# A decoder's state-space scan on one core: who adds the partial sums, products without use, and where the next stage is prepared

## The chip, the cores and the metric

One core of one Trainium2 chip runs the whole program. The metric is the device time of the program in microseconds, as the median of several runs; a profiled execution of the same program gives the trace.

## The reference

The reference is four layers of a decoder over 8 batches of 256 tokens with 128 features. Each layer is attention of some kind, cross attention to a context, and a feed-forward network, each followed by `x = layernorm(x + f(x))`. The change touches two of these twelve stages: the feed-forward network of the second layer (called L1f), and the stage behind it, the state-space model of the third layer (L2a).

L1f is a gated network with dequantised weights:

```
gate = silu(x @ w_gate.T);  up = x @ w_up.T;  y = (gate * up) @ w_down.T
```

L2a, for N = 16 states per feature, computes B and C (16 numbers per token each) and a step size dt (one number per token and feature) from x, and then

```
dt = softplus((x @ W_dt1 + b_dt1) @ W_dt2 + b_dt2)
h[t] = exp(dt[t] * A) * h[t-1] + (the inputs made from x[t] and B[t])
y[t] = sum over the 16 states n of C[t, n] * h[t, n]  + D * x[t]
```

## The kernel before, in words

The program is written by hand for five engines: each engine's instructions stand in one queue in the order of the code, and semaphores join the queues. Nothing reorders them. The functions below are written once per engine; a function named `scan_...` belongs to L2a, wherever it is called.

**The scan (L2a).** The 16 states of a batch are cut into four chunks of four states, so 8 batches give 32 chunks, t = 0 to 31; c = t % 4 is the chunk of a batch. A chunk is 128 features by 4 x 256 tokens. For chunk t:

- ScalarE and GpSimd (`scan_scaled`, GpSimd's line L886) scale the rows of x by B; TensorE (`scan_inputs`, L1891, 8 products) turns and spreads them into PSUM; ScalarE copies the start values over them (`start`, L2636). `scan_inputs(t)` waits until the scan of chunk t-2 has read that bank.
- ScalarE makes the decays (L2626).
- VectorE scans along the tokens (L3524) and multiplies the result in place by C (L3528), which TensorE has spread into PSUM (`spread_c`, L1977). The multiply releases the semaphore `L2a_hc`.
- TensorE (`summed`, L1989) adds the four states of the chunk by four float32 products with the identity into one PSUM bank. For c = 0 a product with the diagonal D comes first (L1987). The scan of chunk t+2 waits for `summed(t)`, since it writes the same tile.

TensorE's loop over t does, in this order: `spread_c(t)`, `summed(t-1)`, then the parts that prepare a later batch or finish an earlier one, then `scan_inputs(t+2)`. The parts are: for t % 4 = 0 `scan_project` (L1870); for 1 `scan_step_sizes` (L1877, L1879); for 2 `result` (L2008) and `cross` (L2000); for 3 `scan_turn_x` (L1859 to L1864). VectorE's loop does the norm of a finished batch (L3554, t % 4 = 0), the softplus (L3451, L3452, t % 4 = 1), scan and multiply of chunk t, then reads y (L3540), `scan_crossed_rows` (L3400, L3402, t % 4 = 0), `scan_sized` (L3410), the series of a logarithm (L3419, L3422; three steps for t % 4 = 3, two for 0) and the statistics of the layer norm (L3545, L3548, t % 4 = 3). GpSimd's loop does `scan_scaled(t+3)`, the first state of a batch (L907, L909), `scan_signed` (L895, L896), and `root` (L918, L919), which gives the rstd that VectorE's norm waits for.

**The gated network (L1f)** runs over b = 0 to 7: two wide products (`gated_widen`, L1915), SiLU on ScalarE (L2591), VectorE's product (L3466), the narrow product (`gated_narrow`, L1925), residual and statistics on VectorE (L3471, L2807 to L2812), rstd and normalised rows on GpSimd (L740, L1054). Between the batches stand pieces that prepare batches 0 and 1 of the scan: VectorE's `scan_constants` for b = 2, which ends with the table SEL of 64 x 2048 elements (L3441) and then releases ScalarE's `scan_projected(0)`; TensorE's `scan_step_sizes(0)` for b = 3 and `scan_step_sizes(1)` for b = 6. The latter waits for VectorE's `scan_crossed_rows(1)`, which stands behind two steps of the series and the softplus. ScalarE's `scan_small_exponential(1)` waits for `scan_sized(1)`.

## Time and profile before

| | us |
|---|---|
| median of 3 runs | 1726.93 |
| lowest and highest of the 3 | 1718.28, 1728.19 |
| the profiled execution's own time | 1728.67 |
| its span, first to last instruction | 1726.8 |
| mean granted TensorE clock | 0.942 |

The span is 1.9 us shorter than the profiled execution's time; the rest lies ahead of the first and behind the last instruction. The scan takes the stretch from about 775 to 958 us of the span, the gated network the one from about 718 to 775.

### The profile page before, as it was taken

What the parts mean: (1) busy time and instruction counts of PE and PEld (TensorE: products, weight loads), DVE (VectorE), ACT (ScalarE), POOL (GpSimd) and SP (SyncE); (2) the same over time, 40 slices, a digit from 0 to 9 for tenths busy, and PEclk for the clock granted to TensorE, in tenths of its full rate; (3) what the DMA queues carried; (4) which work ended last, traced back from release to release, by engine and by line L of the source; (5) the groups of instructions that cost most, each with busy time, mean ns of one, the idle gap of its engine ahead of it and who ended that gap; (6) DMA issues with size and microseconds to landing.
All of it is one profiled execution on the core that took longest, in us unless ns stands there. A gap on an engine that the chain in (4) does not pass through costs nothing.

```text
span 1726.8 us, 34149 instructions
## 1 busy us (share of the span) xinstructions
PE 1509.5 (87%) x12661; PEld 1083.3 (63%) x12661; DVE 1231.5 (71%) x2790; ACT 997.9 (58%) x2035; POOL 594.2 (34%) x800
## 2 busy tenths in 40 slices
PE   6588878789998898789999899998889999989975
PEld 5344436678787555567788667665549984755542
DVE  1688864697776798447888577758844448659888
ACT  4499943367666577356766255547754443157765
POOL 2455535578887021342222223220001111511223
PEclk9799979899999999989999999999988999799985
DMA  3200121200000000000000100000000000000000
GB/s 134 112 14 13 38 93 37 63 10 2 1 1 1 2 2 2 8 14 25 1 1 1 59 2 2 2 13 2 2 2 1 1 10 1 1 19 2 2 1 25
DMA packets 14788, 31.08 MB, mean 18 GB/s; under 512 B 1537, under 2 KB 10017, under 8 KB 13857
## 3 DMA queue, kind: packets, MB, share of 16 engines
q1 hardware_dynamic: 13602, 26.81, 4.5%
q0 software_dynamic: 1024, 2.10, 0.4%
q8 instruction: 103, 1.69, 0.4%
q14 instruction: 59, 0.48, 0.1%
HBM read 22.60 MB, written 6.29 MB: 17 GB/s over the span
## 4 chain that ended last, share of the span: by engine, by line
PE 49%; DVE 13%; POOL 13%; issue 12%; ACT 11%; DMA 1%; SPq 0%; POOLq 0%; DVEq 0%; ACTq 0%
PE PS L1488 5%; PE PS L1541 4%; POOL big L866 4%; ACT big L2361 4%; PE PS L1813 3%; DVE negmax L2938 3%; PE PS L1802 3%; POOL big L854 3%; PE PS L1891 3%; ACT big L2339 2%; PE PS L1989 2%; PE PS L1563 2%; POOL big L862 2%; PE PS L1391 2%; PE PS L1467 2%
## 5 line engine op out<-in xcount | busy, mean ns | idle before, releaser
L2339 ACT ACTIVATE big<-PS 128x1024 f32<-128x1024 f32 (+1 forms) x256 | 249.3, 974 | 157.4 <-PE PS L1495 156.9
L2938 DVE TENSOR_REDUCE negmax<-PS 128x4 f32<-128x1024 f32 x192 | 234.8, 1223 | 57.6 <-PE PS L1488 52.9
L1488 PE MATMUL PS<-KS,QS 32*128 32x256 f32 (+1 forms) x1152 | 133.4, 316 | 33.5 <-DVE negmax L2938 21.0
L1488 PEld LDWEIGHTS PS<-KS,QS 32*128 32x128 f32 x1152 | 87.3, 186 | 106.7 <-ACT big L2339 76.1
L740 POOL TENSOR_TENSOR rstd<-veps,mhalf 128x2 f32<-128x2 f32 x72 | 51.4, 714 | 249.5 <-DVE veps L2812 240.0
L1495 PE MATMUL PS<-QS,KS 32*128 32x256 f32 (+1 forms) x1152 | 133.8, 319 | 1.4 <-ACT big L2339 1.4
L1541 PE MATMUL PS<-big,V 128*32 128x256 f32 (+1 forms) x2048 | 133.6, 379 | 0.3 <-DVE V L3030 0.3
L766 POOL TENSOR_TENSOR res<-resb,XB 128x256 f32<-128x256 f32 x24 | 17.4, 727 | 254.7 <-ACT resb L2425 254.7
L2957 DVE SCALAR_TENSOR_TENSOR QT<-PS,wint 128x1024 f32<-128x1024 f32 x64 | 77.3, 1220 | 17.7 <-PE PS L1433 17.0
L808 POOL TENSOR_SCALAR KT<-QT 128x1024 f32<-128x1024 f32 x64 | 66.6, 1040 | 66.5 <-DVE QT L2957 63.3
L1495 PEld LDWEIGHTS PS<-QS,KS 32*128 32x128 f32 x1152 | 84.7, 187 | 5.5 <-issue 3.7
L2516 ACT ACTIVATE QT<-PS,W 128x256 f32<-128x256 f32 x128 | 53.6, 470 | 55.8 <-PE PS L1802 55.8
L854 POOL TENSOR_SCALAR big<-big,rsum 128x256 f32<-128x256 f32 (+1 forms) x144 | 60.7, 433 | 71.2 <-DVE rsum L2859 70.9
L1537 PE MATMUL PS<-big,V 128*32 128x512 f32 x512 | 64.5, 622 | 22.9 <-ACT big L2361 15.4
L866 POOL TENSOR_TENSOR big<-big 128x512 f32<-128x512 f32 x64 | 81.3, 1270 | 5.0
L1541 PEld LDWEIGHTS PS<-big,V 128*32 128x32 f32 x2048 | 54.2, 110 | 44.1 <-issue 15.4
L1195 PE MATMUL PS<-OT,W 128*128 128x256 f32 x272 | 75.6, 400 | 6.1 <-ACT QT L2287 6.1
L2361 ACT ACTIVATE big<-KT,W 128x1024 f32<-128x1024 f32 x64 | 73.0, 1141 | 9.0 <-POOL KT L808 9.0
L2287 ACT COPY QT<-PS 64x256 f32<-64x256 f32 x128 | 46.8, 366 | 53.4 <-DVE big L2843 51.7
L3524 DVE TENSOR_TENSOR_SCAN V<-big,PS 128x1024 f32<-128x1024 f32 x32 | 73.0, 2281 | 2.9 <-ACT PS L2636 2.4
L2361 ACT ACTIVATE big<-QT,W 128x1024 f32<-128x1024 f32 x64 | 72.8, 1138 | 2.9 <-DVE QT L2957 2.9
L1891 PE MATMUL PS<-W,QT 128*128 128x128 f32 x480 | 62.8, 286 | 9.1 <-DVE V L3524 9.1
(498 smaller groups left out, 4086.4 us busy)
## 6 DMA issues: line engine op xcount, KB each, us to landing
W<-in_wpack SPq DMA_DIRECT2D x1, 4180.0 KB, 14.0
W<-in_wpack SPq DMA_DIRECT2D x1, 2560.0 KB, 8.7
W<-in_wpack SPq DMA_DIRECT2D x1, 2449.5 KB, 9.3
y_rows<-one_more SPq DMA_DIRECT2D x1, 2048.0 KB, 9.4
masks<-in_mask SPq DMA_DIRECT2D x8, 256.0 KB, 2.9
x_rows<-x_tok SPq DMA_DIRECT2D x16, 128.0 KB, 2.0
W<-in_wpack SPq DMA_DIRECT2D x1, 1538.0 KB, 6.4
x_tok<-in_x SPq DMA_DIRECT2D x1, 1024.0 KB, 4.8
```

Source lines behind the costliest of these rows:

```text
L854: ins = nc.gpsimd.tensor_scalar(PRW[:, u % 4, c0:c1], PRW[:, u % 4, c0:c1], rsum[:, u % 16, j:j + 1], 1.0, ALU.mult, ALU.mult)
L866: nc.gpsimd.tensor_tensor(q, q, RTW[:, u % 4, :, :], ALU.add).then_inc(sem("t_rope"), 1)
L1195: mm = nc.tensor.matmul(PS[:, QKB[u % 2], k * S:(k + 1) * S], w(f"{n}_w{x}", h * P, (h + 1) * P), OT[:, b, :], start=True, stop=True)
L1488: mm = nc.tensor.matmul(PS[:, MAXB[half], o], QS[r, bm % 2, tm, j * P:(j + 1) * P], KS[r, bm % 2, tm, k], start=not a.causal, stop=last)
L1495: mm = nc.tensor.matmul(PS[:, exp_banks(ge)[half], o], KS[r, be % 2, te, kb * P:(kb + 1) * P], QS[r, be % 2, te, q], start=not a.causal, s ...
L1541: mm = nc.tensor.matmul(out_rows[:, skip:S], v, PX[:, T % 2, h, kb * S:(kb + 1) * S - skip], start=first, stop=last)
L1891: mm = nc.tensor.matmul(PS[:, bank, first:first + P], chunk("x", t)[:, (k % 2 * 4 + k // 2) * P:(k % 2 * 4 + k // 2 + 1) * P], w("L2a_ahea ...
L2339: nc.scalar.activation(PX[:, T % 2, 2 * p:2 * p + 2, 0:cols], PS[:, exp_banks(g)[0]:exp_banks(g)[0] + 2, 0:cols], ACT.Exp, scale=a.scale). ...
L2361: nc.scalar.activation((PX, PX2)[k][:, T % 2, 2 * p:2 * p + 2, :], clipped((QT, KT)[k], g), ACT.Exp, scale=a.scale, bias=w(("high_base", " ...
L2938: ins = nc.vector.tensor_reduce(negmax[:, h:h + 2, :].rearrange("p h j -> p (h j)"), banks.rearrange("p h (j k) -> p (h j) k", j=2), AX.X, ...
L2957: nc.vector.scalar_tensor_tensor(clipped(QT, g), PS[:, pair_banks(g):pair_banks(g) + 2, :], -100.0 / a.scale, capT[:, g // PAIRS % 2, :].u ...
L3524: nc.vector.tensor_tensor_scan(h, chunk("decay", t), flat(PS[:, bank:bank + 2, :]), 0.0, ALU.mult, ALU.add)\
```

## The change

There are three parts.

1. **Sums.** After its multiply, chunk t is no longer summed by four products. GpSimd adds the second half of the chunk (two states) to the first (`scan_pairs`, a tensor_tensor of 128 x 512 float32), and TensorE's `summed` has two products in place of four. `summed(t-1)` waits for GpSimd's add, and stands behind the preparing parts in TensorE's loop, just ahead of `scan_inputs(t+2)`. For c = 0 it begins with a bfloat16 product of the identity (128 x 256) that writes the unused half of the bank.
2. **Products without use.** `scan_inputs(t)` begins, for t >= 2 except t % 4 = 2, with eight bfloat16 products of 128 x 256 whose result nobody reads, ahead of its waits.
3. **Preparation.** The table SEL is built for b = 4 of the gated network in place of b = 2. The step sizes of batch 1, and what follows from them, go behind the network's own last work on TensorE, VectorE and GpSimd; `scan_crossed_rows(1)` goes ahead of the series for b = 6. GpSimd's `scan_scaled(0)` and `(1)` go behind its rows of b = 5 and b = 6.

The diff (a line of "..." stands where lines are left out):

```
+            def scan_pairs(t):
+
+                pool.wait_ge(sem("L2a_hc"), t + 1)
+                h = chunk("h", t)
+                nc.gpsimd.tensor_tensor(h[:, 0:512], h[:, 0:512], h[:, 512:1024], ALU.add).then_inc(sem("L2a_added"), 1)
...
                     if (b := due(t, SCAN_U, 4)) is not None and b >= 2:
                         scan_signed(b)
+                    if 0 <= t < 4 * B:
+                        scan_pairs(t)
                     if (b := due(t, SCAN_STATS, 4)) is not None and b < B - 1:
                         root(b)
...
                     elif b == 3:
                         scan_signed(0)
-                    elif b == 6:
-                        scan_signed(1)
-                        scan_scaled(0)
-                        scan_scaled(1)
                     inverse_root(n, b)
...
                     ins.then_inc(x_done, 1)
+                    if b in (5, 6):
+                        scan_scaled(b - 5)
+                scan_signed(1)
...
             def scan_inputs(t):
 
+                for _ in range(8 if t >= 2 and t % 4 != 2 else 0):
+                    nc.tensor.matmul(PS[:, 6, S:2 * S], identb[:, :], identb[:, :].unsqueeze(1).broadcast_to([P, 2, P]),
+                                     start=False, stop=False)
                 pe.wait_ge(sem("L2a_xs"), t + 1)
...
-                    elif b in (3, 6):
-                        scan_step_sizes(b // 6)
+                    elif b == 3:
+                        scan_step_sizes(0)
                 pe.wait_ge(sem(f"{n}_silu"), B)
                 scan_inputs(0)
                 gated_narrow(B - 1)
+                scan_step_sizes(1)
                 scan_inputs(1)
...
                 def summed(t):
                     b, c = t // 4, t % 4
-                    pe.wait_ge(sem(f"{n}_hc"), t + 1)
+                    pe.wait_ge(sem(f"{n}_added"), t + 1)
                     if c == 0:
                         if b:
                             pe.wait_ge(sem(f"{n}_y_read"), 2 * b)
-                        nc.tensor.matmul(PS[:, YB, 0:S], diag, xN(b), start=True, stop=False)
-                    for k in range(4):
+                        nc.tensor.matmul(PS[:, YB, S:2 * S], identb[:, :], identb[:, :].unsqueeze(1).broadcast_to([P, 2, P]),
+                                         start=True, stop=False)
+                        nc.tensor.matmul(PS[:, YB, 0:S], diag, xN(b), start=False, stop=False)
+                    for k in range(2):
                         mm = nc.tensor.matmul(PS[:, YB, 0:S], ident, chunk("h", t)[:, k * S:(k + 1) * S],
-                                              start=False, stop=c == 3 and k == 3)
+                                              start=False, stop=c == 3 and k == 1)
...
                     if 0 < t < 4 * B:
                         spread_c(t)
-                    if t:
-                        summed(t - 1)
...
                         scan_turn_x((t + 9) // 4)
+                    if t:
+                        summed(t - 1)
                     if t + 2 < 4 * B:
                         scan_inputs(t + 2)
...
-                line.did(nc.vector.tensor_tensor(SEL[:, :, :], inverse_parts.unsqueeze(1).broadcast_to([64, 16, P]),
-                                                 w("L2a_state", rows=64).unsqueeze(2).broadcast_to([64, 16, P]), ALU.mult))
...
+            def scan_spread():
+                line.wait()
+                line.did(nc.vector.tensor_tensor(SEL[:, :, :], inverse_parts.unsqueeze(1).broadcast_to([64, 16, P]),
+                                                 w("L2a_state", rows=64).unsqueeze(2).broadcast_to([64, 16, P]), ALU.mult))
...
+                    elif b == 4:
+                        scan_spread()
                     elif b == 5:
                         scan_series(0, 0, 3)
                     elif b == 6:
+                        scan_crossed_rows(1)
                         scan_series(0, 3, 5)
                         scan_softplus(0)
-                        scan_crossed_rows(1)
-                        scan_sized(1)
                 gated_residual(B - 1)
+                scan_sized(1)
```

In the printed order below, the lines are those of each kernel's own file: from `scan_pairs` on, the changed file's numbers are higher.

TensorE at the end of the gated network, before: wide products L1915, narrow products L1925, step sizes of batch 1 L1877 and L1879, inputs of the scan L1891.

```order
L1915 MATMUL PS<-QT,big 128x256 x3
L1877 MATMUL PS<-OT,W 128x256
L1879 MATMUL PS<-W,KT 128x16 x2
L1915 MATMUL PS<-QT,big 128x256 x3
L1925 MATMUL PS<-big,QT 128x128 x6
L1915 MATMUL PS<-QT,big 128x256 x3
L1891 MATMUL PS<-W,V 128x128 x8
L1925 MATMUL PS<-big,QT 128x128 x6
L1891 MATMUL PS<-W,V 128x128 x8
```

The same place after; the wide products are L1925, the narrow ones L1935, the step sizes L1884 and L1886, the inputs L1901.

```order
L1925 MATMUL PS<-QT,big 128x256 x6
L1935 MATMUL PS<-big,QT 128x128 x6
L1925 MATMUL PS<-QT,big 128x256 x3
L1901 MATMUL PS<-W,V 128x128 x8
L1935 MATMUL PS<-big,QT 128x128 x6
L1884 MATMUL PS<-OT,W 128x256
L1886 MATMUL PS<-W,KT 128x16 x2
L1901 MATMUL PS<-W,V 128x128 x8
```

The step sizes of batch 1 have moved from between the wide products of batches 6 and 7 to behind the last narrow product.

TensorE in the scan, the iterations t = 1 and 2, before: spreading C is L1977, the diagonal L1987, the sums L1989.

```order
L1977 MATMUL PS<-KS,SEL 128x256 x4
L1987 MATMUL PS<-KT 128x256
L1989 MATMUL PS<-V,W 128x256 x4
L1877 MATMUL PS<-OT,W 128x256
L1879 MATMUL PS<-W,KT 128x16 x2
L1891 MATMUL PS<-W,QT 128x128 x8
L1977 MATMUL PS<-KS,SEL 128x256 x4
L1989 MATMUL PS<-V,W 128x256 x4
L2000 MATMUL PS<-one_more,W 128x256
L1891 MATMUL PS<-W,QT 128x128 x8
```

After, from t = 1 to the inputs issued in t = 2: spreading C is L1988, the diagonal L2000, the sums L2002, the products without use L1893 and L1998, the cross product L2013.

```order
L1988 MATMUL PS<-KS,SEL 128x256 x4
L1884 MATMUL PS<-OT,W 128x256
L1886 MATMUL PS<-W,KT 128x16 x2
L1998 MATMUL PS<-identb 128x256
L2000 MATMUL PS<-KT 128x256
L2002 MATMUL PS<-V,W 128x256 x2
L1893 MATMUL PS<-identb 128x256 x8
L1901 MATMUL PS<-W,QT 128x128 x8
L1988 MATMUL PS<-KS,SEL 128x256 x4
L2013 MATMUL PS<-one_more,W 128x256
L2002 MATMUL PS<-V,W 128x256 x2
L1893 MATMUL PS<-identb 128x256 x8
```

The sums have half their products and stand behind the step sizes or the cross product; eight products without use stand between them and the inputs.

GpSimd in the scan, from the first state of batch 2 on (t = 6), before: first state L907 and L909, signed B L895 and L896, scaled rows L886, the root L918 and L919.

```order
L907 TENSOR_TENSOR KT<-KT 128x16
L909 TENSOR_TENSOR KT<-KT 128x16
L895 TENSOR_SCALAR rsum<-rt,W 128x16
L896 TENSOR_TENSOR sums<-rt,W 2x32
L886 TENSOR_TENSOR QT<-x_tok,rt 128x512
L918 TENSOR_SCALAR veps<-mv 128x2
L919 TENSOR_TENSOR rstd<-veps,mhalf 128x2
L886 TENSOR_TENSOR QT<-x_tok,rt 128x512 x3
```

After, from the same place: the same in lines L913 and L915, L901 and L902, L886, L924 and L925; the new adds are L895.

```order
L913 TENSOR_TENSOR KT<-KT 128x16
L915 TENSOR_TENSOR KT<-KT 128x16
L901 TENSOR_SCALAR rsum<-rt,W 128x16
L902 TENSOR_TENSOR sums<-rt,W 2x32
L895 TENSOR_TENSOR V<-V 128x512
L886 TENSOR_TENSOR QT<-x_tok,rt 128x512
L895 TENSOR_TENSOR V<-V 128x512
L924 TENSOR_SCALAR veps<-mv 128x2
L925 TENSOR_TENSOR rstd<-veps,mhalf 128x2
L886 TENSOR_TENSOR QT<-x_tok,rt 128x512
L895 TENSOR_TENSOR V<-V 128x512
L886 TENSOR_TENSOR QT<-x_tok,rt 128x512
```

An add stands behind every step's scaled rows, and for t % 4 = 3 ahead of the root that VectorE's norm waits for.

## Rows read from the trace of the kernel before

**Rows 1.** Busy time by stretch: length, five engines' busy us, PEclk, DMA share, GB/s.
```profile
754.20:767.00 12.80, 8.59 (x34) 7.27 (x34) 5.30 (x16) 4.73 (x12) 5.19 (x7) 0.73 0.01 1
...
785.00:796.00 11.00, 11.00 (x51) 8.78 (x51) 7.17 (x6) 5.86 (x18) 2.54 (x6) 0.69 0.01 1
796.00:881.00 85.00, 80.73 (x484) 68.00 (x484) 72.00 (x92) 61.60 (x183) 20.40 (x33) 1.00 0.00 1
881.00:890.00 9.00, 8.84 (x48) 7.75 (x48) 6.51 (x7) 5.56 (x16) 1.95 (x5) 0.81 0.00 0
```
**Rows 2.** Timeline of the gated network: start us, us, engine, line, operation [idle before <-releaser].
```profile
728.91 2.28 DVE L3441 TENSOR_TENSOR SEL<-On,W 64x2048 fp32r<-64x2048 f32 x1
...
731.63 0.46 ACT L2551 ACTIVATE one_more<-PS,W 16x256 f32<-16x256 f32 x1 [8.40 <-DVEq L3445]
...
736.40 1.19 PE L1877 MATMUL PS<-OT,W 64*128 64x256 f32 x2 [4.95 <-DVE one_more L3402]
...
748.38 0.42 DVE L3471 TENSOR_TENSOR res<-PS,x_tok 128x256 f32<-128x256 f32 x1 [2.88 <-PE PS L1925]
...
758.42 1.05 PE L1877 MATMUL PS<-OT,W 64*128 64x256 f32 x2 [4.21 <-DVE one_more L3402]
...
763.93 0.47 ACT L2561 ACTIVATE KT<-PS,W 128x256 f32<-128x256 f32 x1
```
**Rows 3.** Timeline ahead of the first scan.
```profile
771.38 1.26 ACT L2583 ACTIVATE QT<-x_tok,rt 128x128 f32<-128x128 f32 x4
...
774.19 0.22 POOL L907 TENSOR_TENSOR KT<-KT 128x16 f32<-128x16 f32 x1
...
774.79 0.17 ACT L2636 COPY PS<-KT 128x8 f32<-128x8 f32 x1 [2.15 <-POOL KT L909]
...
775.16 2.29 DVE L3524 TENSOR_TENSOR_SCAN V<-big,PS 128x1024 f32<-128x1024 f32 x1 [2.38 <-ACT PS L2636]
```
**Rows 4.** Timeline of one batch of the scan.
```profile
819.41 1.22 DVE L3528 TENSOR_TENSOR V<-V,PS 128x1024 f32<-128x1024 f32 x1
...
823.81 0.61 DVE L3554 SCALAR_TENSOR_TENSOR x_tok<-res,mv,rstd 128x128 f32<-128x128 f32 x2 [1.12 <-POOL rstd L919]
...
824.33 0.73 PE L1977 MATMUL PS<-KS,SEL 64*128 64x256 f32 x4
...
828.92 0.47 DVE L3400 SCALAR_TENSOR_TENSOR KS<-PS,W,KS 32x256 fp32r<-32x256 f32 x1 [0.71 <-ACT OT L2553]
...
832.08 2.29 DVE L3524 TENSOR_TENSOR_SCAN V<-big,PS 128x1024 f32<-128x1024 f32 x1
...
834.51 2.02 PE L1891 MATMUL PS<-W,QT 128*128 128x128 f32 x16 [1.11 <-DVE V L3524]
...
836.47 0.73 PE L1977 MATMUL PS<-KS,SEL 64*128 64x256 f32 x4
...
837.13 1.99 PE L1989 MATMUL PS<-V,W 128*128 128x256 f32 x8
...
838.96 0.38 PE L2008 MATMUL PS<-W,XB 128*128 128x128 f32 x2
...
841.88 0.73 PE L1977 MATMUL PS<-KS,SEL 64*128 64x256 f32 x4
...
842.72 1.22 DVE L3528 TENSOR_TENSOR V<-V,PS 128x1024 f32<-128x1024 f32 x1
```
**Rows 5.** By line: ns min/median/max, first and last start, forms.
```profile
L1786 PE MATMUL PS<-causal,identb x40: 270/272/273, 309.5 to 313.8; 128*128 128x256 bf16 x40
...
L866 POOL TENSOR_TENSOR big<-big x64: 1260/1268/1328, 332.3 to 549.7; 128x512 f32<-128x512 f32 x64
```
**Rows 6.** VectorE's softplus by line, and its one slow case on the timeline.
```profile
L3451 DVE SCALAR_TENSOR_TENSOR OT<-OT,xs x8: 424/425/1220, 756.3 to 923.9; 128x256 f32<-128x256 f32 x8
...
923.76 1.04 POOL L886 TENSOR_TENSOR QT<-x_tok,rt 128x512 f32<-128x512 f32 x1 [3.61 <-PE PS L1891]
923.86 1.22 DVE L3451 SCALAR_TENSOR_TENSOR OT<-OT,xs 128x256 f32<-128x256 f32 x1
```

## The prediction

> **What bounds the kernel now.** I read the timeline of the stretch that the change touches, then the busy time by stretch, and then the timeline again, ahead of the scan.
>
> The scan comes first. One batch of it, four chunks, repeats every 23.3 us, and the timeline shows what holds the period [rows 4]. TensorE's iteration t % 4 = 0 begins at 824.33 with the spread of C; ScalarE, once TensorE's inputs are through, needs until 828.92 before VectorE can begin the crossed rows (it waited 0.71 for ScalarE): 4.6. From there VectorE does series and softplus and starts the scan at 832.08 (3.2), TensorE's inputs wait 1.11 for that scan and start at 834.51 (2.4), take 1.96 to the next spread at 836.47, and from there TensorE works without a pause: 5.4 to the spread at 841.88, then 5.8 to the same point of the next batch. The sum is 23.3. So TensorE is the bound in two iterations out of four, and ScalarE and VectorE are in the other two. VectorE itself has little to spare: from the end of its multiply of chunk 3 (819.41 + 1.22 = 820.63) to its next scan it needs 3.7, 1.12 of it a wait for GpSimd's rstd; only the 0.71 ahead of L3400 is slack.
>
> The clock is the second view [rows 1]. In 796 to 881 TensorE had 1.00 of its clock; in 785 to 796 it had 0.69 and in 881 to 890 0.81, with TensorE busy throughout. The first stretch follows a wait for the scan, and so does the second; each such wait is 1.1 us long, as the one at 834.51.
>
> The third view is the gated network [rows 2]. TensorE stood 4.95 us ahead of the step sizes of batch 0 at 736.40, and 4.21 us ahead of those of batch 1 at 758.42, both for VectorE's L3402. After the second it ran at 0.73 [rows 1]. The first scan at 775.16 waited for ScalarE's start copy, which had waited 2.15 for GpSimd's first state [rows 3].
>
> **The change part by part.**
>
> *The table SEL.* ScalarE's L2551 is released by VectorE's queue behind the table and one short instruction (8.40 of wait) [rows 2]. The table takes 2.28. With it gone from b = 2, the chain ScalarE, crossed rows, step sizes comes 2.3 sooner, and so does all that follows in the gated network. For b = 4 the table lies ahead of L3471 at 748.38, where VectorE idled 2.88: that hides it. Without that cover it would cost the 2.3 again. I take -2.3; bounds -2.3 and 0.
>
> *Batch 1's step sizes.* TensorE no longer stands 4.2 in the middle of the network, so the last rows are normalised sooner, and GpSimd's first state with them. What is late next is ScalarE: its queue before the first scan ended at 771.38 + 1.26 = 772.64 [rows 3]. That queue hangs on `scan_small_exponential(1)`, which still waits for the step sizes of batch 1. Before, ScalarE came to it at 763.93 [rows 2]. In the new order TensorE has, from 754.20 on, wide, narrow, wide, inputs(0), narrow and the step sizes: two wide pairs and the inputs of 1.96 [rows 4] and the rest come, as an estimate, to 8 to 9 us at full clock, and one wait for VectorE's product to about 1. That is 763.2 to 764.2, the time of before: the saved wait and the saved half clock pay for the work placed ahead. So the start copy goes from 774.79 to about 772.9: -1.9. Bounds: 0, where another wait takes its place, and -4.2, the whole wait. GpSimd's scaled rows (1.04 each) go behind rows of b = 5 and 6 and are wanted later than they end; `scan_signed(1)` lands ahead of the first state, in the 2.15 that ScalarE has to spare. Neither costs anything.
>
> *Sums and products without use.* Four sums take 838.96 - 837.13 = 1.83 [rows 4]; two take 0.92, so 0.91 is saved per chunk. A bfloat16 product of 128 x 256 comes every (313.8 - 309.5)/39 = 0.11 [rows 5]; eight take 0.88. In the iterations t % 4 = 2 and 3, which bind, one replaces the other: -0.03 each. For t % 4 = 1 the products lie in the 1.11 of wait. For t % 4 = 0 there are none, and 0.91 is saved, but the inputs wait for the scan there and the path goes by ScalarE's 4.6 anyway. The projection moves ahead of the sums, which ScalarE sees by less than 0.1. So per batch -0.1, over 6 batches -0.6; bounds -1.2 and 0. The new wait, for GpSimd's add: the add takes 1.27 [rows 5], with semaphores 1.4 behind the multiply. For t % 4 = 2 TensorE comes to its sums 1.6 after its spread began and more than 2 us behind the multiply, for 3 later still; it doesn't wait. Queued behind the waiting sums are only the useless products and the inputs. `scan(t+2)` waits for the sums, which come 1 us and more before it.
>
> *GpSimd against VectorE.* The 1.27 of GpSimd is not free. VectorE's softplus step takes 0.425, but 1.22 at 923.86, where it started 0.10 behind GpSimd's L886 (1.04): it ended 0.28 behind it [rows 6]. Both of its operands are in SBUF. After the multiply for t % 4 = 3 VectorE goes on with three such steps of the series, and GpSimd's add starts at that very moment. I count 1.27 of delay there, ahead of statistics, rstd and norm. Slack is 0.71, so 0.6 per batch is left. This hits the five batches in which series and statistics are both there: +3.0. Bounds: 0 if they don't collide; 1.7 per batch if GpSimd's next scaled rows (1.04) also get in ahead of VectorE's norm, +8.5. I take the value nearest to the row. The Trainium skill, "SBUF — State Buffer", section on who interferes with whom, says that a VectorE instruction with two SBUF inputs and a reading GpSimd instruction exclude each other for their whole length; the trace agrees, with 1.22 against 0.425. By that rule alone the term would lie between 3.0 and 8.5.
>
> *The end of the scan.* Behind the last multiply stand now an add (1.27, and 0.1 for its semaphore) and two sums in place of four: 1.37 - 0.91 = +0.45. I take +0.4; bounds -1, as the last cross product comes sooner, and +1.
>
> *The clock.* TensorE lost 11 x 0.31 = 3.4 us in 785 to 796 and 9 x 0.19 = 1.7 in 881 to 890 [rows 1], 5.1 in all. The products without use shorten the wait at 834.51 from 1.1 to below 0.9, while a wait of about 1.7 opens for t % 4 = 0, where there are none. I take half back, -2.5; bounds -5.1 and +5.
>
> The sum: -2.3 - 1.9 - 0.6 + 3.0 + 0.4 - 2.5 = -3.9. The profiled execution took 1728.67, so 1724.8 for the like of it. That execution lies 1.7 above the median of 1726.93; against the median I get 1723.0.
>
> **The rivals.**
>
> *No collision, and the clock holds.* GpSimd's add falls between VectorE's steps, and both slow stretches go: -2.3 - 1.9 - 0.6 + 0.4 - 5.1 = -9.5, so 1717.4. For it: products are placed just where TensorE waited at 834.51. Against it: the slow case of L3451.
>
> *The preparation gains nothing.* Another wait ahead of the first scan takes the place of the one removed, so -3.9 + 4.2 = +0.3: 1727.2. For it: ScalarE's chain hangs on step sizes that the change puts later. Against it: the 2.28 stands plainly on the chain.
>
> *GpSimd stretches VectorE's path until TensorE falls to half clock.* Its place is t % 4 = 3 and 0. If both collisions fall in each batch, VectorE's path grows by 2.3, the period by 1.7, and TensorE then waits 2.7 us for the scan with no products there. From the point where such a wait drops the clock as the two before did, each of 6 batches pays like 785 to 796 did, up to 3.4. That is 8.5 + 20.4, with -2.3 - 1.9 - 0.6 + 0.4 from the rest, +24.5: 1751.4. For it: 1.1 us of wait was followed by half clock twice. Against it: the same 1.1 us stood in the other batches at 1.00.
>
> **How the numbers follow.** My forecast 0.45, the first rival 0.24, the second 0.23, the third 0.08. A measurement of this kernel tells about 1% (17 us) from no change. The forecast and the first two rivals all lie within 1%, but the runs of the kernel before spread over 10 us, so the first rival gives part of its chance to faster: faster 0.10, same 0.82, slower 0.08. The range: the first rival less the 8.6 between the median and the lowest run gives 1709; upward, the forecast's own collisions at their upper bound (+5.5) and the clock at its (+7.5) give 1736.
>
> **What would show it.** Right: the step sizes of batch 0 start 2.3 sooner with TensorE's wait near 2.7; the first scan starts near 771; the add takes 1.27; a VectorE series step behind the multiply of t % 4 = 3 takes over 1 us; the period is 23.8 to 24.0. Wrong: a period of 23.2 (no collision) or above 24.5; TensorE's clock below 1.00 in every batch; the table SEL on the chain for b = 4; TensorE waiting for GpSimd ahead of its sums.

## The result and the profile after

The changed kernel took 1736.53 us as the median of 12 runs (1725.01 to 1745.49), the kernel before 1723.94 in 12 runs on the same chip (1716.62 to 1732.75). The ratio is 1.0065, with a 95% interval of 1.0038 to 1.0092: slower by 7 to 16 us, where I had forecast 3.9 us faster. The time itself lies 0.5 us above the range's upper end of 1736.

The profiled execution took 1736.52 us with a span of 1734.8. From the page of the changed kernel, its head and TensorE's line:

```profile
span 1734.8 us, 34283 instructions
...
PE 1502.0 (87%) x12707; PEld 1075.7 (62%) x12717; DVE 1244.1 (72%) x2790; ACT 996.7 (57%) x2035; POOL 635.9 (37%) x832
```

TensorE has less to do than before and VectorE more, though VectorE has the same 2790 instructions: some of them got longer. To see where, I cut the span at three events that both programs have: GpSimd's first normalised rows in the gated network, the first scan, and the end of VectorE's last multiply.

| us | before | after |
|---|---|---|
| first rows of the network to first scan | 54.7 | 51.9 |
| first scan to end of last multiply | 181.0 | 185.6 |
| from there to the end (other stages) | 770.6 | 775.9 |

The preparation gained 2.8 and the scan lost 4.6 in this execution (7.9 in a second one of the same kernel, e9 below). The last piece is the same code in both, and over the executions profiled in this study it varies from 755 to 776 by itself: it took 755 at a mean granted clock of 0.97 and 775 at 0.93. Little can be read from it but its first microseconds, below.

The timeline of the changed kernel, one batch of the scan (the iterations that answer to [rows 4]; the multiply for t % 4 = 3 is the first row):

```profile
840.14 1.22 DVE L3546 TENSOR_TENSOR V<-V,PS 128x1024 f32<-128x1024 f32 x1 [0.24 <-PE PS L1988]
...
841.28 0.42 DVE L3432 SCALAR_TENSOR_TENSOR xs<-OT 128x256 f32<-128x256 f32 x1
...
841.44 1.39 POOL L895 TENSOR_TENSOR V<-V 128x512 f32<-128x512 f32 x1 [0.94 <-DVE V L3546]
841.73 1.84 DVE L3435 SCALAR_TENSOR_TENSOR xs<-masks,xs 128x256 f32<-128x256 f32 x2
...
844.75 0.71 POOL L925 TENSOR_TENSOR rstd<-veps,mhalf 128x2 f32<-128x2 f32 x1
...
845.43 1.04 POOL L886 TENSOR_TENSOR QT<-x_tok,rt 128x512 f32<-128x512 f32 x1
845.49 1.39 DVE L3572 SCALAR_TENSOR_TENSOR x_tok<-res,mv,rstd 128x128 f32<-128x128 f32 x2 [1.11 <-POOL rstd L925]
...
846.80 2.27 DVE L3542 TENSOR_TENSOR_SCAN V<-big,PS 128x1024 f32<-128x1024 f32 x1
...
849.22 2.02 PE L1901 MATMUL PS<-W,QT 128*128 128x128 f32 x16 [1.97 <-DVE V L3542]
...
871.62 2.27 DVE L3542 TENSOR_TENSOR_SCAN V<-big,PS 128x1024 f32<-128x1024 f32 x1
```

GpSimd's add starts 0.16 behind VectorE's first series step, and the two steps after it take 1.84 in place of 0.88. The norm, which took 0.61 in [rows 4], takes 1.39, with GpSimd's scaled rows started 0.06 ahead of it. VectorE needs 5.4 us from the end of its multiply (841.36) to its next scan, where it needed 3.7, and TensorE then waits 1.97 for that scan. Scans of the same chunk number stand 24.8 us apart (846.80 and 871.62), where they stood 23.3 apart.

From the end of the scan of the changed kernel:

```profile
957.73 1.22 DVE L3546 TENSOR_TENSOR V<-V,PS 128x1024 f32<-128x1024 f32 x1
...
959.03 1.26 POOL L895 TENSOR_TENSOR V<-V 128x512 f32<-128x512 f32 x1 [3.13 <-DVE V L3546]
...
960.34 1.42 PE L2002 MATMUL PS<-V,W 128*128 128x256 f32 x4 [3.26 <-POOL V L895]
...
965.00 2.08 PE L1354 MATMUL PS<-ctxT,W 128*128 128x256 f32 x4
```

TensorE stands 3.26 us for the last multiply and the last add behind it, and what follows runs at the granted clock of 0.5, which is 1.2 GHz: L1354 takes 2.08. The same four products, L1347 of the kernel before, took 1.13:

```profile
960.40 1.13 PE L1347 MATMUL PS<-ctxT,W 128*128 128x256 f32 x4
```

They started 4.2 us behind the end of the last multiply before, and 6.1 us after the change.

### The profile page after: what moved, and what is told of

Read it like the earlier page. It is cut to its first block, busy times and chain, and to the rows that moved or that the text cites. A ratio compares the mean times of both kernels' runs of the same rounds, so it can differ in the third digit from the quotient of the medians.

```text
span 1734.8 us, 34283 instructions
## 1 busy us (share of the span) xinstructions
PE 1502.0 (87%) x12707; PEld 1075.7 (62%) x12717; DVE 1244.1 (72%) x2790; ACT 996.7 (57%) x2035; POOL 635.9 (37%) x832
## 4 chain that ended last, share of the span: by engine, by line
PE 49%; DVE 13%; POOL 12%; ACT 12%; issue 11%; another core or an unknown queue 1%; DMA 1%; SPq 0%; POOLq 0%; DVEq 0%; ACTq 0%
PE PS L1495 5%; PE PS L1548 4%; ACT big L2374 4%; POOL big L866 4%; PE PS L1820 3%; PE PS L1901 3%; DVE negmax L2951 3%; PE PS L1809 3%; POOL big L854 3%; ACT big L2352 2%; POOL big L862 2%; PE PS L1570 2%; PE PS L1398 2%; PE PS L1474 2%; PE PS L1462 2%
## 5 line engine op out<-in xcount | busy, mean ns | idle before, releaser
L1901 PE MATMUL PS<-W,QT 128*128 128x128 f32 x480 | 65.6, 295 | 18.1 <-DVE V L3542 18.1
L1901 PEld LDWEIGHTS PS<-W,QT 128*128 128x128 f32 x480 | 62.0, 209 | 22.6 <-issue 22.3
```

The lines of the kernel that those rows point to most:

```text
L1901: mm = nc.tensor.matmul(PS[:, bank, first:first + P], chunk("x", t)[:, (k % 2 * 4 + k // 2) * P:(k % 2 * 4 + k // 2 + 1) * P], w("L2a_ahea ...
```

## The experiments

The theory: GpSimd's instructions that read SBUF and VectorE's instructions with two operands in SBUF exclude each other, and the add puts one such pair into every batch, and a second by what it delays. The rivals: the products without use cost the time; the wait for the add costs it; the clock; the preparation itself.

All results together. "Network" and "scan" are the first two pieces of the table above, from each kernel's profiled execution; "batch" is the distance of two scans of the same chunk number, four chunks apart, in the batches of the middle of the scan with the clock at 1.00; e2 and e4 have no such batch, and theirs is the usual distance, at a clock of 0.93. Ratios are against the kernel before on the same chip; e5 and e6 were executed once, and their whole times tell nothing here.

| | ratio, interval | network | scan | batch |
|---|---|---|---|---|
| before | 1 | 54.7 | 181.0 | 23.3 |
| the change | 1.0065, 1.0038 to 1.0092 | 51.9 | 185.6 | 24.8 |
| e1 preparation only | 0.9947, 0.992 to 0.9973 | 51.9 | 180.3 | 23.3 |
| e2 sums only | 1.002, 0.9993 to 1.0047 | 54.7 | 183.9 | 24.5 (at 0.93) |
| e3 products only | 1.0015, 0.9989 to 1.0041 | 54.8 | 187.4 | 24.9 |
| e4 change without products | 1.0013, 0.9982 to 1.0043 | 50.3 | 189.4 | 24.5 (at 0.93) |
| e5 idle reading instruction | one run | 54.7 | 192.4 | 24.5 |
| e6 idle memset | one run | 56.3 | 179.3 | 23.3 |
| e7 adds apart | 0.9998, 0.9975 to 1.0021 | 51.5 | 176.8 | 22.9 |
| e8 preparation, late sums | 0.9959, 0.9932 to 0.9986 | 51.9 | 177.0 | 23.2 |
| e9 the change again | 1.0048, 1.0023 to 1.0074 | 51.9 | 188.9 | 24.8 |
| e10 change, adds apart | 0.9986, 0.9954 to 1.0018 | 51.9 | 181.2 | 23.2 |
| e12 step sizes only | 1.0015, 0.9993 to 1.0037 | 54.0 | 180.2 | 23.3 |
| e13 waits filled | 0.9958, 0.9926 to 0.9989 | 51.5 | 172.8 | 22.9 |
| e14 table only | 0.9993, 0.9958 to 1.0028 | 52.5 | 181.1 | 23.3 |

### The three parts, each alone, and the change without the second

e1 takes `scan_pairs`, the later place of `summed` and the products out of the change. e2 keeps only these sums; e3 puts only the eight products into the kernel before; e4 takes them out of the change:

```
-                for _ in range(8 if t >= 2 and t % 4 != 2 else 0):
-                    nc.tensor.matmul(PS[:, 6, S:2 * S], identb[:, :], identb[:, :].unsqueeze(1).broadcast_to([P, 2, P]),
-                                     start=False, stop=False)
```

> Only part 3 (preparation) on the kernel before; sums and products as before. Theory (the sums on GpSimd collide with VectorE and make the change slow): the batches of the scan repeat every 23.3 us again, the first scan starts 2 to 4 us sooner than before, and the kernel is 2 to 4 us faster than before. Rival (the preparation itself loses, since the table SEL holds GpSimd off its normalised rows): the first scan starts no sooner than before, and the kernel is 0 to 3 us slower than before.

> Only part 1 (GpSimd adds halves, two sums, later in TensorE's order), no products without use, preparation as before. Theory of the collision: VectorE's series steps and norm are still stretched (about 1.8 for two series steps in place of 0.9, 1.4 for the norm in place of 0.6), and the period is 24 to 25 us though TensorE has 2.6 us less to do in it; 5 to 12 us slower than before. Rival (the products without use cost the time, as TensorE was the bound): the period falls to about 22 us and the kernel is 8 us or more faster than before.

> Only part 2 (eight products without use ahead of the inputs' waits), sums and preparation as before. TensorE binds two iterations of four in the kernel before, so by the theory each gets 0.88 longer: the period grows from 23.3 to about 25.0, and the kernel is 8 to 14 us slower than before, less up to 5 if the clock then never falls in the scan. Rival (they lie in waits): the period stays 23.3 and the kernel is the same or up to 5 us faster.

> The changed kernel without part 2. Theory of the collision (VectorE is the bound of the changed kernel): the period falls by less than 0.5 from 24.8 us in spite of 2.6 us less work for TensorE; within 4 us of the changed kernel, so 7 to 15 us slower than before. Rival (the products are what costs): the period falls by 1.5 or more and the kernel is 2 us or more faster than before. By the clock as a rival: TensorE's clock falls in most batches and the kernel is more than 20 us slower than before.

The preparation alone is faster: the network's piece is 2.8 shorter, and the batch is 23.3. Its 5 to 14 us in the whole kernel are more than I expected and more than the 3.5 that its two pieces account for; what the rest is stays open.

The sums alone stretch the batch to 24.5, with less work for TensorE. From 820 us on the clock falls once in every batch there: over its scan e2 had 0.92 where the kernel before had 0.97 (below). In the whole kernel e2 is between 1 us faster and 8 us slower than before, where I expected 5 to 12 slower. The products alone give 24.9, which is 23.3 and twice 0.8: as costed, they lie on TensorE's path in two iterations of four. I expected the whole kernel 8 to 14 us slower, less up to 5 for the clock; it is between 2 us faster and 7 us slower. The scan of the profiled execution is 6.4 us longer, at a clock of 1.00, and that lies within this interval.

e4 takes the products out of the change, and the batch goes from 24.8 to 24.5, by less than 0.5 as the theory has it: with both collisions left, 2.6 us less work for TensorE brings 0.3. But e4's clock falls in every batch from 805 on, so what it would take at full clock isn't shown. One distance in e2 (827.15 to 850.93) and one in e4 are 23.8. In the one of e2 TensorE's inputs took 3.75 at half clock, so that GpSimd's next scaled rows came behind VectorE's softplus, whose two steps took 0.42 each:

```profile
846.63 3.75 PE L1899 MATMUL PS<-W,QT 128*128 128x128 f32 x16 [3.50 <-DVE V L3534]
...
850.02 0.42 DVE L3461 SCALAR_TENSOR_TENSOR OT<-OT,xs 128x256 f32<-128x256 f32 x1
...
850.48 0.42 DVE L3462 SCALAR_TENSOR_TENSOR KT<-OT,KT 128x256 f32<-128x256 f32 x1
850.53 1.27 POOL L886 TENSOR_TENSOR QT<-x_tok,rt 128x512 f32<-128x512 f32 x1 [1.45 <-PE PS L1899]
```

In the next two batches one of the two steps takes 1.15: a third collision. From the scan of chunk 0 to that of chunk 1 it is 7.4 us there, and 6.7 where the softplus went free.

In the whole kernel e4 doesn't behave as expected. I had it 7 to 15 us slower than before; it is between 3 us faster and 7 us slower (1.0013), less than the change in its two measurements (1.0065 and 1.0048), though the intervals overlap. So it isn't excluded by the whole times that the products have a part in what the change costs. And the scan of e4's profiled execution, 189.4, is no shorter than the change's, at a clock of 0.88.

The busy time by stretch over the scan, of before, e2, e3 and e7 (columns as in [rows 1]):

```profile
775.16:956.20 181.04, 170.64 (x996) 142.62 (x994) 151.63 (x180) 118.72 (x354) 41.88 (x68) 0.97 0.03 10
```
```profile
773.60:957.50 183.90, 149.96 (x880) 125.75 (x878) 163.69 (x180) 117.34 (x354) 82.19 (x99) 0.92 0.03 9
```
```profile
772.80:960.20 187.40, 183.46 (x1172) 154.23 (x1170) 151.22 (x180) 118.48 (x354) 42.13 (x68) 1.00 0.03 10
```
```profile
767.90:944.70 176.80, 151.70 (x904) 127.38 (x904) 155.31 (x180) 117.81 (x354) 70.44 (x90) 0.95 0.00 1
```

VectorE's busy time is the figure behind TensorE's two, and the clock is the one behind GpSimd's. VectorE has 180 instructions in all four. They take 151.6 and 151.2 without the add, and 163.7 with it: 12 us more for the same work. TensorE's busy time goes the other way, and in these four the clock follows TensorE's: 1.00 in e3, where it hardly rests, and 0.92 in e2, where it rests most.

### The disputed cost by itself

Both kernels are the one before, with one more instruction on GpSimd at the place of the add. Nobody waits for it, and its output is read by nobody. e5 adds the identity to itself and so reads SBUF:

```
+                    if 0 <= t < 4 * B:
+                        if t:
+                            pool.wait_ge(sem("junk"), t)
+                        pool.wait_ge(sem("L2a_hc"), t + 1)
+                        nc.gpsimd.tensor_tensor(wint[:, 0:512].bitcast(F32).rearrange("p (a b) -> p a b", a=4), ident.unsqueeze(1).broadcast_to([P, 4, P]), ident.unsqueeze(1).broadcast_to([P, 4, P]), ALU.add).then_inc(sem("junk"), 1)
```

e6 has a memset there, long enough to take the same time, which reads nothing:

```
+                    if 0 <= t < 4 * B:
+                        if t:
+                            pool.wait_ge(sem("junk"), t)
+                        pool.wait_ge(sem("L2a_hc"), t + 1)
+                        nc.gpsimd.memset(wint[:, 0:1152].bitcast(F32), 0.0).then_inc(sem("junk"), 1)
```

> The kernel before, with one more GpSimd instruction behind each multiply: a tensor_tensor of 128 x 512 float32 that reads two operands in SBUF and writes where nobody reads. No engine waits for it. Theory of the collision: it alone stretches VectorE's two series steps behind the multiply of t % 4 = 3 from 0.88 to about 1.8, and the batches repeat every 23.8 to 24.8 us in place of 23.3. Rival (the new wait for the sum is what costs, not the instruction): 23.3 us, series steps 0.88.

> The same, but the instruction is a memset of about the same length, which reads nothing. Theory, as a reading collision (two SBUF inputs of VectorE against a reading GpSimd): series steps stay at 0.88 and the period at 23.3 us. Rival (any GpSimd instruction on SBUF collides, or its place in GpSimd's queue costs): as with the reading one, 23.8 us or more.

The timeline of e5, behind the multiply for t % 4 = 3:

```profile
845.48 0.42 DVE L3424 SCALAR_TENSOR_TENSOR xs<-OT 128x256 f32<-128x256 f32 x1
845.71 1.09 POOL L934 TENSOR_TENSOR wint<-W 128x512 f32<-128x512 f32 x1 [1.01 <-DVE V L3533]
845.93 1.60 DVE L3427 SCALAR_TENSOR_TENSOR xs<-masks,xs 128x256 f32<-128x256 f32 x2
...
849.42 1.04 POOL L886 TENSOR_TENSOR QT<-x_tok,rt 128x512 f32<-128x512 f32 x1
849.45 1.42 DVE L3559 SCALAR_TENSOR_TENSOR x_tok<-res,mv,rstd 128x128 f32<-128x128 f32 x2 [1.11 <-POOL rstd L919]
```

And of e6, at the same place:

```profile
842.41 0.42 DVE L3424 SCALAR_TENSOR_TENSOR xs<-OT 128x256 f32<-128x256 f32 x1
842.62 1.06 POOL L934 MEMSET wint<- 128x1152 f32 x1 [0.99 <-DVE V L3533]
842.87 0.89 DVE L3427 SCALAR_TENSOR_TENSOR xs<-masks,xs 128x256 f32<-128x256 f32 x2
...
845.68 0.62 DVE L3559 SCALAR_TENSOR_TENSOR x_tok<-res,mv,rstd 128x128 f32<-128x128 f32 x2 [1.12 <-POOL rstd L919]
```

An instruction on GpSimd that no engine waits for stretches the batch from 23.3 to 24.5, and one of the same length at the same place that reads nothing leaves it at 23.3 to the hundredth (23.32). Each is one execution, but its batches at full clock agree within 0.03. The two series steps take 1.60 beside the read and 0.89 beside the memset. So it is not the wait for the sum, and not the place in GpSimd's queue; it is that GpSimd reads. e5 also shows the second collision: the first has delayed the norm until GpSimd's scaled rows are free to start, and they get in just ahead of it. The Trainium skill, "SBUF — State Buffer", section on who interferes with whom, says that a VectorE instruction with two SBUF inputs contends with a GpSimd instruction that reads SBUF, and not with one that only writes it, and that the contention is an exclusive lock. Both runs agree, with 1.60 beside the read and 0.89 beside the memset.

### The collision taken out

e7 is the change without the products, with the sum of chunk 3 by four products again, and with one wait on GpSimd, ahead of the scaled rows for t % 4 = 0, for VectorE's norm. e10 is the same with all the products of the change kept. e9 is the change itself, and e8 has the preparation and the later place of the four sums:

```
-                    if 0 <= t < 4 * B:
+                    if 0 <= t < 4 * B and t % 4 in (0, 1, 2):
                         scan_pairs(t)
...
+                    if (b := due(t, SCAN_DONE, 4)) is not None and b < B - 1:
+                        pool.wait_ge(x_done, base[n] + b + 1)
                     if 2 <= t + 3 < 4 * B:
                         scan_scaled(t + 3)
```

> The changed kernel without products without use, with GpSimd's add for chunks 0, 1 and 2 of a batch only (chunk 3 has its four sums), and GpSimd's scaled rows for t % 4 = 0 held until VectorE's norm is through. Theory of the collision: series steps 0.88 and norm 0.61 again, TensorE has 2.7 us less to do per batch than before and VectorE loses little, so the period falls to 22 to 23 us and the kernel is 8 to 16 us faster than before. Rival (the bound is elsewhere, with the clock): a period above 23.3 us, and no faster than the preparation alone.

> The preparation, and of part 1 only the later place of the sums in TensorE's order: four sums per chunk, no add on GpSimd, no products without use. By my steps the later place is worth less than 0.2 us per batch: period 23.1 to 23.3, within 2 us of the preparation alone. Rival (the later place of the sums itself delays the scan of chunk t+2): period above 23.6.

> The changed kernel itself, on the same chip as the next three. From its first measurement, 0.4 to 0.9% slower than before, with a period of 24.8 us at full clock.

> The changed kernel with all its products without use, but GpSimd's add for chunks 0, 1 and 2 of a batch only, and GpSimd's scaled rows for t % 4 = 0 held until VectorE's norm is through. Theory (the collision with VectorE is what made the change slow): the period falls from 24.8 to 23.1 to 23.5 us, where TensorE binds, and the kernel is 8 to 15 us faster than the changed one. Rival (the products without use are what costs, the collision lies beside them): period above 24.3 us, within 4 us of the changed one.

e10 against e9 is the cleanest comparison. From e10, the norm of one batch and the two scans of chunk 0 around it:

```profile
863.04 0.88 DVE L3441 SCALAR_TENSOR_TENSOR xs<-masks,xs 128x256 f32<-128x256 f32 x2
...
865.83 0.61 DVE L3578 SCALAR_TENSOR_TENSOR x_tok<-res,mv,rstd 128x128 f32<-128x128 f32 x2 [1.10 <-POOL rstd L925]
866.36 2.28 DVE L3548 TENSOR_TENSOR_SCAN V<-big,PS 128x1024 f32<-128x1024 f32 x1
866.56 1.04 POOL L886 TENSOR_TENSOR QT<-x_tok,rt 128x512 f32<-128x512 f32 x1 [0.76 <-DVE x_tok L3578]
...
889.60 2.28 DVE L3548 TENSOR_TENSOR_SCAN V<-big,PS 128x1024 f32<-128x1024 f32 x1
```

The series steps take 0.88 and the norm 0.61 again. The batch falls from 24.8 to 23.23, which is what e8 gives with no add at all, and the ratios go from 1.0048 to 0.9986, which is 11 us (4 to 18 with both intervals). So the first two collisions together cost 1.6 us per batch; the two weren't taken out one at a time. Six batches of that are 9.6 us, of the 15 to 20 by which the change is behind the preparation alone (e8 and e1). e8 gives 23.2: the later place of the sums is worth the 0.1 that I had costed. e7 gives the 22.9 that was expected, in batches at full clock, and yet no gain in the whole kernel (within 4 us of before), where I expected 8 to 16 us. Its timeline shows a part of why: in four batches TensorE, relieved, stands 2.36 to 2.97 and then runs the inputs at 1.2 GHz, 3.5 to 3.7 us long:

```profile
845.34 3.65 PE L1900 MATMUL PS<-W,QT 128*128 128x128 f32 x16 [2.36 <-DVE V L3545]
```

Such batches take 24.0 to 24.2, though one more, with the same wait of 2.36 at 822.45, kept its full clock. In the scan a part of the work taken off TensorE came back as half clock. It isn't the whole account: the two pieces of the profiled execution are still 7.6 us shorter than before, and why the median of 12 runs shows nothing of that stays open.

### The waits filled, and the preparation taken apart

e13 is e7 with eight products without use in two places, ahead of the sums for t % 4 = 0 and ahead of the inputs for t % 4 = 1:

```
+                    for _ in range(8 if t and t % 4 == 0 else 0):
+                        nc.tensor.matmul(PS[:, 6, S:2 * S], identb[:, :], identb[:, :].unsqueeze(1).broadcast_to([P, 2, P]),
+                                         start=False, stop=False)
                     if t:
                         summed(t - 1)
```

e12 leaves the table SEL at b = 2, e14 moves only the table. A kernel with the products ahead of the inputs for t % 4 = 0 and 1 alone (e11) gave no result.

> Of the preparation only the later step sizes of batch 1 and what goes with them; the table SEL is built for b = 2 as before; sums as before, no products without use. By my steps the first scan then starts about 2 us sooner than before and 2.3 us later than with the whole preparation, less what SEL costs GpSimd at its new place (up to 1.8). Rival (the table's new place brings nothing): it starts as soon as with the whole preparation, and the kernel is as fast.

> The kernel of e7 (preparation, adds for chunks 0 to 2 only, norm ahead of the scaled rows) with eight products without use in two places of four: ahead of the sums for t % 4 = 0 and ahead of the inputs for t % 4 = 1, where TensorE waits for the scan. Theory (in e7 the clock gave the gain back): TensorE's clock is 1.00 in all of the scan, every batch takes 22.8 to 23.0 us, and from the first scan to the last multiply it is 173 to 175 us in place of 176.8 in e7 and 181.0 before; 8 to 14 us faster than before. Rival (they don't hold the clock, or cost TensorE's path): batches of 24 us and more as in e7, or all of 23.7 us; within 5 us of before.

> The kernel before with only the table SEL moved to b = 4. Theory: from the network's first rows to the first scan 52.5 us (2.3 less than before's 54.8), as e1 (51.9) and e12 (54.1) leave it; GpSimd's rows of b = 3 take about 3.4 in place of 1.57 beside it. Rival (the table hides nothing by itself, and only both parts together gain): 54 us or more. In the whole kernel 2 us, about what can just be told from nothing.

e13's batches are 22.86 to 22.90 through the middle of the scan, at full clock behind the same places where e7's fell, and its scan takes 172.8, the shortest; with the network's piece that is 11.5 us less than before. So in the scan the clock took 3.9 us from e7. In the whole kernel e13 is 2 to 13 us faster than before, which can't be told from e1 and e8; e7 was measured on another chip, and its interval meets this one, so that the clock took e7's gain in the whole kernel is likely but not shown. Of the preparation's 2.8 us the table gives 2.3 (e14) and the step sizes 0.7 (e12, a miss: I expected 2). The whole times of e12 and e14 can't be told from before. In e14 GpSimd's rows beside the table:

```profile
745.23 3.25 POOL L1054 TENSOR_SCALAR x_tok<-res,mv,rstd 128x128 f32<-128x128 f32 x2
745.46 2.35 DVE L3447 TENSOR_TENSOR SEL<-On,W 64x2048 fp32r<-64x2048 f32 x1
748.58 0.42 DVE L3474 TENSOR_TENSOR res<-PS,x_tok 128x256 f32<-128x256 f32 x1 [0.77 <-POOL x_tok L1054]
```

GpSimd's two instructions, which take 1.57 together elsewhere, take 3.25, and VectorE's residual then waits 0.77 for them: the collision works both ways. The table's cover was there, but it was not only VectorE's.

## Why the prediction was wrong

**The step that failed** is the one headed "GpSimd against VectorE". Its mechanism was right and named, its size was not. I took 0.6 per batch in five batches, "the value nearest to the row", and put the second collision, at 1.7 per batch, into the upper bound. (By the prediction's own figures both come to 1.27 + 1.04 - 0.71 = 1.6, so the bound of +8.5 should have been +8.0.) e10 against the change measures 24.82 - 23.23 = 1.6 per batch, and the norm takes 1.39 or more in six batches: the second collision falls in every one of them, and the term is 9.6 where I had 3.0. It could have been seen. In [rows 4] TensorE's spread at 824.33 marks the end of the inputs that release GpSimd's scaled rows, and GpSimd's rstd had ended 0.6 ahead of that:

```profile
823.05 0.72 POOL L919 TENSOR_TENSOR rstd<-veps,mhalf 128x2 f32<-128x2 f32 x1
...
824.49 1.04 POOL L886 TENSOR_TENSOR QT<-x_tok,rt 128x512 f32<-128x512 f32 x1 [0.71 <-PE PS L1891]
```

The rows stood ready 0.7 behind the rstd, and the norm, which takes 0.61, just fitted in between. The first collision delays the rstd by about 1 us, more than that gap; then the rows are ready when the rstd ends, and they start with it, ahead of the norm. There is a third collision, that I had not listed. In this batch, behind inputs at half clock, it is on the softplus:

```profile
828.18 1.04 POOL L886 TENSOR_TENSOR QT<-x_tok,rt 128x512 f32<-128x512 f32 x1 [1.34 <-PE PS L1901]
...
828.24 1.27 DVE L3468 SCALAR_TENSOR_TENSOR KT<-OT,KT 128x256 f32<-128x256 f32 x1
```

At full clock it falls on a series step (1.27 for 0.43 at 851.69). It is in e13's batches of 22.9 too, so it isn't what makes the 24.8.

**The table, -2.3:** right. e14 measures 2.3, and in the changed kernel TensorE's wait for the step sizes of batch 0 went from 4.95 to 2.67 as said.

**Batch 1's step sizes, -1.9:** 0.7 (e12). ScalarE was late next, as said. But its chain didn't come 2.3 sooner. It came to L2574, the answer to L2561 of [rows 2], at 764.33. Reckoned from the network's first rows (720.4 before, 721.4 after), that is 43.0 against 43.5, 0.5 sooner. And I had put GpSimd's moved rows at nothing; they collide:

```profile
755.97 1.84 DVE L3435 SCALAR_TENSOR_TENSOR xs<-masks,xs 128x256 f32<-128x256 f32 x2
...
756.48 1.04 POOL L886 TENSOR_TENSOR V<-x_tok,rt 128x512 f32<-128x512 f32 x1
...
761.13 1.60 PE L1935 MATMUL PS<-big,QT 128*128 128x128 f32 x12 [1.44 <-DVE QT L3482]
```

The series steps lose about 0.9 there, ahead of VectorE's product, for which TensorE's last narrow product waits 1.44 where I had allowed about 1.

**Sums and products, -0.1 per batch:** right. e10 and e8 give 23.23 and 23.22 for 23.32, and e3 shows the products' price where nothing was taken away for them. TensorE waited for the add nowhere within the scan by more than 0.2 us, but at its end.

**The end, +0.4:** too small. The same four products of the next stage start 1.9 later behind the last multiply (6.1 for 4.2), the last sums having waited 3.26. The sums themselves start 1.39 behind the multiply in place of 0.05, as costed; what I had not costed is that TensorE runs at half clock behind a wait of that length.

**The clock, -2.5:** the second step that failed, with the wrong sign. Counted as the prediction counts it, half clock lost 5.1 us in the scan before, and 10.2 in the changed kernel: +5.1. Over the scan the clock was 0.97 before and, in the changed kernel:

```profile
773.30:958.90 185.60, 164.46 (x1052) 137.39 (x1052) 164.55 (x180) 117.83 (x354) 79.91 (x97) 0.94 0.00 1
```

The inputs ran in 3.1 to 3.8 us in place of 2.02 behind waits of 0.97, 1.97, 1.95 and 2.75, and in 2.02 behind five others of 1.5 to 2.2. The new wait of 1.7 for t % 4 = 0, which I had seen coming, came as 1.97.

With these measured terms the prediction's sum is -2.8 - 0.6 + 9.6 + 1.9 + 5.1 = +13.2, within the 7 to 16 us measured. That is a check of size and no more: lost clock isn't all on the path, and the two profiled scans of the changed kernel were 4.6 and 7.9 us longer than before, less than these terms add up to.

The rival that ended on the slower side had the mechanism and both collisions, and too high a price: the clock fell in some batches, not in all six. That the time came out beside the range's upper end says nothing for the forecast: that bound added two terms at their worst. What I weighed wrongly between it and the forecast was the step from "bounded above by the second collision" to "the second collision follows from the first".

## What to carry to other kernels

Before work goes to GpSimd, list for each of its new instructions which VectorE instructions with two SBUF operands stand beside it, and after adding the first delay list them again: a collision moves the schedule into the next one. Where the moved work relieves an engine that isn't alone on the loop, ask what its new rest does to its clock; a product without use is free only ahead of a wait that the trace shows, and costs its full length in an iteration without one (sixteen of them cost 1.6 us per batch in e3). The parts of a change should be run apart: here one was 0.5% faster alone, and the whole hid it.

## What the runs showed of the hardware that I had not expected

The lock between the two engines can pass between two VectorE instructions of one queue: GpSimd's add started 0.16 behind the first series step and took 1.39 in place of 1.27, and the second step, which started 0.03 behind the first one's end, ended 0.28 behind the add (1.38 for 0.43). So it went in all six batches with an add, a series and a norm. It holds against GpSimd too: beside the table of 2.35 one GpSimd instruction took 2.47 in place of 0.80, so that the two together took 3.25 (e14) and 3.42 (the changed kernel) for 1.57.

TensorE's clock went from 2.4 to 1.2 GHz behind waits as short as 1.1 us, and stayed up behind others of 2.4: the kernel before's 1.11 at 881.16 was followed by the fall (inputs of 3.48 us for 2.02), the same 1.11 at 834.51 and 857.84 was not, and neither was e7's 2.36 at 822.45. So the length of the one wait doesn't decide it.
